# A graph network, linear attention and expert layer on one core: a rebuilt opening, token-major denominators, rotating sum banks

## The reference

```
xn = layernorm(x)
x  = x + gnn(xn) + mix(xn)
x  = x + ffn(layernorm(x))

gnn: xg = layernorm(xn) * norm_g + norm_b
     out1 = gat(xg, W1, 4 heads x 192);  out2 = gat(out1, W2, 2 heads x 96)
     return concat(xn, out2) @ Wu + bu
gat: h = x @ W;  e = leaky_relu(h.a_src[src] + h.a_dst[dst]);  softmax over the edges of each dst
     out[dst] = sum(alpha * h[src]) + bias
mix: q, k = elu(xn @ Wq + bq) + 1, elu(xn @ Wk + bk) + 1;  v = xn @ Wv + bv   (12 heads of 64)
     kv = sum_n k v;  z = 1 / (q . sum_n k);  return (q kv z) @ Wo + bo
ffn: top 2 of 8 experts, each 768 -> 384 -> 768 with gelu, weighted by the gate scores
```

## Time and profile before

| | us |
|---|---|
| three runs | 1069.29, 1074.53, 1076.05 |
| median of the runs | 1074.53 |
| profiled execution, its own time | 1070.59 |
| its span in the profile | 1068.8 |
| mean granted PE clock | 0.948 of 2.4 GHz |
| PE busy | 933.8 (87%) |
| DVE busy | 774.0 (72%) |
| ACT busy | 344.1 (32%) |

### The profile page before, as it was taken

The page is one execution under the profiler, slowest core; times in us unless marked ns, Lnnn a source line. Parts: engine busy times, 40 slices in busy tenths (PEclk is TensorE's granted clock), DMA queues, the critical chain, the costliest instruction groups (busy, mean ns, idle before and its releaser), DMA issues.

```text
span 1068.8 us, 16945 instructions
## 1 busy us (share of the span) xinstructions
PE 933.8 (87%) x6241; PEld 675.4 (63%) x6241; DVE 774.0 (72%) x1740; ACT 344.1 (32%) x424; POOL 134.6 (13%) x139
## 2 busy tenths in 40 slices
PE   3699999999889899979978988967888569999994
PEld 2666666666454455546668988947775446666662
DVE  6568789897765786986587987689989944444442
ACT  3561122122225232432332433314435532222220
POOL 3010000000001000000000000000601035555541
PEclk9889999999999999999989999988899779999997
DMA  8340222135352745627787100006026757778761
GB/s 236 121 163 11 80 66 77 66 121 222 134 193 84 247 163 185 210 84 240 237 330 317 50 1 1 1 1 264 3 92 256 271 179 176 189 186 192 188 165 18
DMA packets 61451, 155.44 MB, mean 145 GB/s; under 512 B 11940, under 2 KB 31270, under 8 KB 58426
## 3 DMA queue, kind: packets, MB, share of 16 engines
q1 hardware_dynamic: 48586, 112.33, 30.1%
q0 software_dynamic: 9936, 34.23, 13.0%
q10 hardware_dynamic: 2848, 7.77, 1.9%
HBM read 108.34 MB, written 48.94 MB: 147 GB/s over the span
## 4 chain that ended last, share of the span: by engine, by line
PE 65%; DVE 22%; DMA 4%; issue 4%; ACT 2%; DVEq 1%; SPq 1%; POOLq 0%
PE PS L1774 40%; PE PS L2017 13%; DVE arena L1517 3%; DVE arena L1473 3%; PE PS L1850 3%; DVE arena L1479 2%; PE PS L2168 2%; PE PS L1830 1%; DVE arena L1489 1%; DVE arena L1379 1%; DMA arena<-in_L_gnn_W_dram 1%; DMA arena<-as_d 1%; PE PS L1861 1%; DVE arena L1275 1%; DVE arena L1223 1%
## 5 line engine op out<-in xcount | busy, mean ns | idle before, releaser
L1774 PE MATMUL PS<-arena 128*128 128x384 f16 (+7 forms) x3396 | 564.6, 322 | 4.8 <-DVE arena L1764 3.0
L1774 PEld LDWEIGHTS PS<-arena 128*128 128x128 f16 (+2 forms) x3396 | 320.7, 99 | 214.3 <-issue 13.5
L2017 PE MATMUL PS<-arena 128*128 128x193 f32 (+1 forms) x1200 | 191.4, 323 | 21.9 <-DVE arena L1479 16.5
L2017 PEld LDWEIGHTS PS<-arena 128*128 128x128 f32 x1200 | 186.9, 200 | 26.4 <-DVE arena L1479 16.0
L1033 ACT ACTIVATE arena<-arena,AS 128x1280 f32<-128x1280 f32 x60 | 81.8, 1363 | 134.9 <-DVE arena L1473 134.7
L1473 DVE SCALAR_TENSOR_TENSOR arena<-arena,AS 128x1280 f32<-128x1280 f32 x60 | 94.2, 1573 | 0.0
L1479 DVE SCALAR_TENSOR_TENSOR arena<-arena 128x1280 f32<-128x1280 f32 x60 | 90.6, 1510 | 3.4 <-PE PS L2017 3.3
L1275 DVE TENSOR_SCALAR arena<-arena 128x240 f16<-128x240 f16 x324 | 89.2, 275 | 0.0
L1274 DVE TENSOR_SCALAR arena<-arena 128x128 f16<-128x128 f16 x324 | 80.2, 248 | 0.1
L1763 DVE SCALAR_TENSOR_TENSOR arena<-PS,arena 128x768 f32<-128x768 f32 x27 | 25.8, 957 | 62.1 <-PE PS L1774 62.1
L1110 ACT ACTIVATE arena<-PS 128x1536 f16<-128x1536 f16 x27 | 39.1, 1449 | 75.7 <-PE PS L2168 75.7
(11 more groups left out here) (268 smaller groups left out, 915.2 us busy)
## 6 DMA issues: line engine op xcount, KB each, us to landing
arena<-in_L_ffn_W_dram SPq DMA_DIRECT2D x48, 384.0 KB, 3.8
fr_d<-arena SPq DMA_DIRECT2D x48, 384.0 KB, 3.5
arena<-fr_d SPq DMA_DIRECT2D x16, 1152.0 KB, 14.5
arena<-in_x_dram SPq DMA_DIRECT2D x18, 384.0 KB, 5.4
arena<-rr_d SPq DMA_DIRECT2D x4, 1280.0 KB, 8.0
g_d<-arena SPq DMA_DIRECT2D x10, 388.0 KB, 2.5
acc_d<-arena SPq DMA_DIRECT2D x10, 384.0 KB, 2.6
xf_d<-arena ACTq DMA_DIRECT2D x10, 384.0 KB, 3.2
```

The costliest lines, as they stand in the source:

```text
L1774: m = T.matmul(out, left[i][x], right[i][y], start=first and i + r == 0, stop=last and 3 * i + r == n - 1)
L2017: m = T.matmul(ps[b][:, r * (C + 1):(r + 1) * (C + 1)], PT[i % deep][:, d * P:(d + 1) * P], feats, start=t == 0 and r == 0, stop=t == NT - ...
```

## The change

In words:

- SP issues W1's first half before it waits for anything, then the edges, x tile 0, W1's second half, x tile 1, W2 with the logit vectors, x tiles 2 and 3, the small columns, Wk, and tiles 4 to 9.
- POOL makes the constants first, then blanks `CT`, then writes the identity on its diagonal (DVE did that at line 1181).
- PE turns W1 in eight groups, four per half, ahead of the window keys, and makes first products 0 to 3 around the keys and the others four ahead of the turned tiles. The bias products are spread: two after every second tile, the last two inside K's first tile. They use banks 6 and 7, the first products banks 4 and 5.
- ACT loads its table for the square root at the start; DVE takes statistics of two tiles ahead of the keys, not four.
- Every split of Wk, Wv, Wq and Wu is made in CUTS = 3 pieces.
- Denominators token-major: the six steps multiply a 128x128 block of Q (left operand) with two columns (`kcol`), so a chunk's result is [128 tokens x (tiles x 12)]; DVE takes the reciprocal of that, splits it in three bf16 parts, PE turns them (`den_turned`) and DVE copies them to `rparts`. The maxima of a chunk's last step move behind it.
- The sums of layer 1 use banks (5 h + b) mod 8 for head h, and `head_result` comes one unit later.

The core of the diff:

```
@@ sync
+            w1_half(0, s_w1_in)
             sp.wait_ge(s_edges_blank, 1)
...
-            for t in range(4):
-                x_tile(t)
-            sp.dma_start(W1S, W1.rearrange("(k p) n -> p k n", p=P)).then_inc(s_w1_in, 16)
-            for t in range(4, XS):
-                x_tile(t)
+            x_tile(0)
+            w1_half(1, s_w1b_in)
+            x_tile(1)
             sp.dma_start(W2A[:, :, 0:CW], W2.rearrange("(k p) n -> p k n", p=KS)).then_inc(s_w2_in, 16)
...
+            for t in range(2, 4):
+                x_tile(t)
...
             weight(0, Wk)
-            for t in range(XS, NT):
+            for t in range(4, NT):
                 x_tile(t)
-            sp.wait_ge(s_stage_low, 1)
+            sp.wait_ge(s_stage_low, CUTS)
             weight(1, Wv)
@@ gpsimd
-            g.memset(reg(O_X, NT * DCOL // 2), 0.0).then_inc(s_ct_blank, 1)
             const(g.memset(ident[:, :], 0.0))
...
             const(g.memset(zrow, 0.0))
+            g.memset(reg(O_X, NT * DCOL // 2), 0.0).then_inc(s_ct_blank, 1)
+            pool.wait_ge(s_ct_blank, 1)
+            for t in range(NT):
+                i = g.tensor_copy(CT[:, t, t * P:(t + 1) * P], ident[:, :])
+            i.then_inc(s_ct_blank, 1)
@@ scalar
+            for t in range(NT):
+                if t + 2 < NT:
+                    std(t + 2)
+                xn_high(t)
+                if t + 2 < NT:
+                    normed(t + 2)
+                if t + AHEAD < 2 * KC:
+                    m_out(t + AHEAD)
+                if 4 <= t < 4 + CUTS:
+                    high(0, t - 4)
@@ vector
+            for t in range(NT):
+                if t + 3 < NT:
+                    row_stats(t + 3)
+                if t + 2 < NT:
+                    inverse(t + 2)
+                if t + 3 < NT:
+                    variance(t + 3)
+                if t + 2 < NT:
+                    shift(t + 2)
+                if t == 0:
+                    dve.wait_ge(s_window_psum, 2)
+                    V.tensor_copy(kc[:, 0, :, :], ps[6][:, 0:EJ * NU]...).then_inc(s_keys_ready, 1)
+                if 5 <= t < 5 + CUTS:
+                    stage_low(0, t - 5)
...
                 if t == 0:
-                    stage_low(1)
+                    for q in range(CUTS):
+                        stage_low(1, q)
...
-            for j in range(KC):
-                V.tensor_scalar(kones[:, j, :], kones[:, j, :], ksum[:, j:j + 1], None, ALU.mult)
+            for half in range(2):
+                s = slice(64 * half, 64 * half + 64)
+                V.tensor_copy(kcol[s, :, half], ksum[s, :])
...
-                for c in conv_of_t[t0]:
-                    conv_low(c)
-                dve.wait_ge(s_den_psum, n + 1)
-                link(V.reciprocal(recip[:, 0:w], ps[2][:, 0:w]))
-                link(V.tensor_copy(rparts[:, 0:w], recip[:, 0:w]))
...
+                dve.wait_ge(s_den_psum, 2 * n + 1)
+                heads = recip[:, 0:nt, :]
+                link(V.reciprocal(heads, ps[2][:, 0:nt * 2 * KC]...))
+                for r in range(3):
+                    part = rcols[:, 0:nt, 2 * KC * r:2 * KC * (r + 1)]
+                    k = V.tensor_copy(part, heads)
+                    if r < 2:
+                        link(k)
+                        link(V.tensor_tensor(heads, heads, part, ALU.subtract))
+                k.then_inc(s_den_ready, 1)
+                for c in conv_of_t[t0]:
+                    conv_low(c)
+                maxima1(late_maxima[0:1])
+                dve.wait_ge(s_den_psum, 2 * n + 2)
+                V.tensor_copy(rparts[:, 0:w], ps[2].bitcast(BF16)[:, 2 * P:2 * P + w]).then_inc(s_den_ready, 1)
+                maxima1(late_maxima[1:])
...
-                    if t == 1 and h:
+                    if t == 2 and h:
                         head_result(h - 1, CW, 0)
@@ tensor
+            for t in range(NT):
+                turned(t)
+                if t + AHEAD < 2 * KC:
+                    first_product(t + AHEAD)
+                if t == 0:
+                    pe.wait_ge(s_keys_ready, 2)
+                    pe.wait_ge(s_small_in, 80)
+                if t % 2:
+                    norm_bias(t // 2)
...
-                m = T.matmul(ps[2][:, 0:w], kones[:, j, :], QT[:, j, 0:w], start=j == 0, stop=j == KC - 1)
+                for t in range(w // P):
+                    at_t = 2 * KC * t + 2 * j
+                    m = T.matmul(ps[2][:, at_t:at_t + 2], QT[:, j, t * P:(t + 1) * P], kcol[:, j, :], start=True, stop=True, ...)
...
+            def den_turned(n):
+                pe.wait_ge(s_den_ready, 2 * n + 1)
+                for t in range(CH[n][1] // P):
+                    m = T.transpose(ps[2].bitcast(BF16)[:, (2 + t) * P:(3 + t) * P], rcols[:, t, :], identb[:, :])
+                m.then_inc(s_den_psum, 1)
...
                     if t == 0 and r == 0 and h:
-                        pe.wait_ge(s_head_out, 5 * (results + h - 1) + b + 1)
-                    m = T.matmul(ps[b][:, r * (C + 1):(r + 1) * (C + 1)], PT[i % deep][:, d * P:(d + 1) * P], feats,
+                        if C != CW:
+                            pe.wait_ge(s_head_out, 5 * (H1 + h - 1) + b + 1)
+                        elif b >= 3:
+                            pe.wait_ge(s_head_out, 5 * (h - 1) + b - 2)
+                        elif h >= 2:
+                            pe.wait_ge(s_head_out, 5 * (h - 2) + b + 3)
+                    m = T.matmul(ps[sum_bank(h, b) if C == CW else b][:, r * (C + 1):(r + 1) * (C + 1)], PT[i % deep][:, d * P:(d + 1) * P], feats,
```

More of the change, by code:

```diff
@@ L529, in group_of, with sum_bank @@
             return [t < b for _, b in GROUPS].index(True)
-        def copies_of(s):
-            return range(s - 4, s - 3) if s < NT + 2 else range(2 * s - NT - 6, 2 * s - NT - 4)
         def rows_bank(i):
             return 5 if i == 1 else 0
+        def sum_bank(h, b):
+            return (5 * h + b) % 8
         def turn_bank(t):
@@ L771, in _ @@
             select(g.memset(bd, 0.0))
-            select(g.memset(kones, 0.0))
-            heads = kones.rearrange("p j (g m) -> p j g m", g=4)
-            for j in range(KC):
-                for half in range(2):
-                    i = g.memset(heads[64 * half:64 * half + 64, j, :, 2 * j + half:32:12], 1.0)
-            select(i)
+            select(g.memset(kcol, 0.0))
+            select(g.memset(rcols, 0.0))
             pool.wait_ge(s_small_in, 96)
@@ L929, in _ @@
             act.wait_ge(s_keys_ready, 2)
-            high(1)
+            for q in range(CUTS):
+                high(1, q)
             for t in range(NT):
@@ L973, in _ @@
                 if t == 3:
-                    high(2)
+                    for q in range(CUTS):
+                        high(2, q)
                 for c in conv_of_g[t]:
@@ L1003, in mask_half @@
                              ACT.Relu, bias=bigc[:, :], scale=-BIG).then_inc(s_mask_ready, 1)
-            high(3)
+            for q in range(CUTS):
+                high(3, q)
             for n, (c0, w) in enumerate(CH):
@@ L1164, in _ @@
             row_stats(0)
-            for s in range(1, 4):
-                row_stats(s)
-                variance(s - 1)
-            inverse(0)
-            variance(3)
-            shift(0)
-            inverse(1)
-            shift(1)
+            row_stats(1)
+            variance(0)
+            variance(1)
             dve.wait_ge(s_const_ready, CONST)
             dve.wait_ge(s_window_psum, 1)
-            V.tensor_copy(kc[:, 1, :, :], ps[5][:, 0:EJ * NU].rearrange("p (j u) -> p j u", j=EJ))
+            V.tensor_copy(kc[:, 1, :, :], ps[7][:, 0:EJ * NU].rearrange("p (j u) -> p j u", j=EJ))
             link(V.tensor_copy(ebase[0:1, :], ps[6][0:1, 0:NU]))
@@ L1178, in _ @@
             V.tensor_copy(lefti[0:1, 0:1], left[0:1, 0:1]).then_inc(s_left_ready, 1)
-            dve.wait_ge(s_ct_blank, 1)
-            for t in range(NT):
-                i = V.tensor_copy(CT[:, t, t * P:(t + 1) * P], ident[:, :])
-            link(i)
+            inverse(0)
+            inverse(1)
+            shift(0)
+            shift(1)
+            row_stats(2)
+            variance(2)
+            dve.wait_ge(s_ct_blank, 2)
             dve.wait_ge(s_left_ready, 1)
@@ L1339, in _ @@
                 if t in (5, 6, 7):
[L1340 to L1345 removed]
+                    stage_low(2, t - 5)
                 for c in conv_of_g[t]:
@@ L1400, in _ @@
                     if i == 0:
-                        stage_low(3)
+                        for q in range(CUTS):
+                            stage_low(3, q)
                     for c in conv_of_j[i]:
@@ L1482, in head_result @@
                 dve.wait_ge(s_agg, unit0 + (h + 1) * NT)
-                acc = PS[:, 0:5 * 512].rearrange("p (a b) -> p a b", a=5)
-                link(V.reciprocal(rden[:, :, :], acc[:, :, C:2 * C + 2:C + 1]))
+                acc = PS.rearrange("p (a b) -> p a b", a=8)
+                first = sum_bank(h, 0) if C == CW else 0
```

(13 more changed lines are left out.)

184 lines of the change are left out of this document (83 added, 101 removed).

## The result

| | before | after |
|---|---|---|
| four runs, median (us) | 1072.69 | 1042.78 |
| lowest and highest | 1069.29, 1076.05 | 1040.11, 1044.75 |
| profiled execution, its span | 1070.59, 1068.8 | 1042.59, 1040.8 |
| mean granted clock | 0.948 | 0.943 |

The ratio is 0.9715, with a 95% interval of 0.9691 to 0.9738: 29.9 us less by the medians, 28.0 less between the two profiled executions. The forecast was 1045.5.

What follows compares the result with a forecast made beforehand. PE was taken to bound the kernel (65% of the span, DVE 22%), leaving its idle and low-clock time to win. 6.0 + 1.0 + 5.9 + 2.1 - 0.1 + 9.8 + 2.4 = 27.1 us, from 1072.6 to 1045.5 us; range 1037 to 1057.

Steps and rivals of the forecast that it cites:

- Opening, 6.0: Opening up to the K bias: it begins at 73.8 instead of 80.64, 6.8 us less 0.8, so 6.0 us won.
- so I add 0.8: Opening, ahead of the turned tiles: 0.8 us added for a low clock after PE's idle 4 to 5 us.
- 11.8 us after Wv's issue: Opening, behind Wv: bias rows and columns are in 11.8 us after Wv's issue, 65.8 for an issue at 54.
- the same sum gave 75.9: Opening, K bias: the same sum for the kernel before gave 75.9, with the bias waited on for PE until 80.64.
- Head selectors, 1.0: Head selectors on DVE: six operations of 1.26 us become two small copies, 1.0 us won (0 to 1.2).
- Denominators, 5.9 + 2.1 - 0.1: Denominators: PE's waits ahead of the shared products go, winning 5.9 us in chunk 0, 2.1 in chunk 1, -0.1 in chunk 2.
- rival (d): Denominators: each small product waits for the one ahead, eating 28 us; 1073.5 and above, chance 0.02.
- Rotating banks, 9.8 + 2.4: Layer 1's changes of head: three pauses of 3.25 us go, 9.8 us, plus 2.4 us counted for low clock.
- rival (b): Head change: DVE misses its 0.2 us reserve for unit 2; heads give 6, not 12.2: 1051.7, chance 0.08.
- (a): Opening gives nothing: Wv's issue comes at 60 and the K bias again at 80; 1051.5, chance 0.14.
- (c): Opening, x tiles: the clock stays at its lower level, 20 us on top; 1066, chance 0.04.
- The exclusive lock: Opening, edge work: POOL's blanking blocks DVE's first edge operation until 10.6; with ports only shared, 2 us earlier.

Runs made afterwards that it cites:

- e10: Changed kernel with 12 and 30 unused identity transposes filling PE's two pauses ahead of the keys; 1040.12 us.
- e4: Changed kernel with the two bias rows and two bias columns issued ahead of Wv instead of behind it; 1039.94 us.
- e1: Changed kernel with the whole denominator change undone (feature-major, long reciprocal, maxima of the last step ahead), selectors undone too; 1055.46 us.
- e8: Changed kernel with its small denominators, but maxima of a chunk's last step and the conversions ahead of the reciprocal again; 1048.91 us.
- e9: Changed kernel with the old feature-major denominators and long reciprocal, but conversions and maxima kept behind the reciprocal; 1051.09 us.
- e3: Changed kernel with rotating banks kept, but the head result after the second unit as before, not the third; 1058.59 us.
- e5: Changed kernel with POOL's blanking of the histogram ahead of the constants again, as in the kernel before; 1044.59 us.
- e6: Changed kernel with POOL's blanking of the histogram cut into ten pieces; 1044.69 us.
- e11: Changed kernel with bias rows and columns issued early, Wv loaded in thirds, and POOL's blanking ahead of the constants; 1035.65 us.
- e12: Changed kernel with bias rows and columns early, Wv in thirds, unused filler transposes on PE, and Wk's splits spread out; 1032.69 us.

## Why the prediction was right, step by step

The sum said 27.1; the two profiled executions differ by 28.0 and the medians by 29.9.

- **Opening, 6.0: too much, it was 4.1.** Right were W1's transposes (begun at 6.47), the hold by POOL (until 10.0, forecast 10.6), tiles at 5.26 us a pair and ACT's 3.6 us in tiles 4 to 6. The edge work ended at 16.5 and the keys came at 24.4, earlier than the forecast 18.0 and 26.4. The low clock, for which "so I add 0.8" stands, cost more: it was at 0.50 to 0.53 from 18 to 32 us, and products 2 and 3 took 5.3 us instead of 2.7; e10 shows its price. The two errors cancel, and the turned tiles began at 30.3, as the sum had it (29.6 and 0.8). What was too small lies behind: from there to Wv's issue it took 25.2 us and not 23.6 (24.4 in e10), and "11.8 us after Wv's issue" was 13.0, since the column b2 was issued 2.5 us behind Wv and landed at 68.6. So the K bias stood at 76.55 and not 73.8. Of these 2.8 us 0.8 came back: the V product for which it had been taken off took 3.08 us, the length at the full clock. That this landing was what DVE waited for, as the prediction put it, e4 shows.
- **The opening's check and its spread.** The check by the kernel before, "the same sum gave 75.9", was none: 52.64 and 19.8 make 72.4, and there DVE's one-hots waited for the last x tiles (until 67.5 us), not for the landing. By the five other traces of this opening the gain is 3.7 to 5.6 us, so up to 1.5 of the missing 1.9 may be chance.
- **Head selectors, 1.0:** 0.8; the two copies are one row of 0.34 us.
- **Splits elsewhere, 0:** nothing separates them in the trace. Not tried alone.
- **Denominators, 5.9 + 2.1 - 0.1:** 6.0 and 2.4 in the trace; 5.3 and 2.6 when undone in e1. The eight records of four small products take 0.95 us (row 347.00) for the 0.92 that line 2048 gave, so rival (d) is out. What the prediction had not seen: the reserve is 1.9 us (copy done at 355.94, used at 357.83), and in chunk 0 the order of the maxima is worth as much as the small reciprocal (e8, e9).
- **Rotating banks, 9.8 + 2.4:** the pauses as said, 3.3 us each in e3. Layer 1 is 14.2 us shorter, so the clock gave 4.4, and 2.4 were counted. 1.3 of the 4.4 come from a place that was left out, a low stretch at the start of layer 1, which cost 2.6 us before (544 to 552) and 1.3 after (530 to 534); the other 3.1 lie within the bound of 3.4. The reserve of 0.2 us for unit 2 was real (0.04 at 604.72), and rival (b) came close.
- **Not in the sum:** two stretches of low clock, 1.7 us each, at 292 and 326. They went though PE's work and waits in those places are the same. Every one of the twelve other variants has at least one of the two, and e1, e5, e6 and e10 have both. One at 466 is new and took 1.7. So 1.7 us net and the 2.0 more in layer 1 stood in for the 1.9 missing in the opening and for what was lost behind layer 1 (1.4): the mechanisms came as told, and that the total fits to 1 us is luck in part.
- **Rivals:** (a) did not come, though 2 us of it did. (c) did not: the clock was at 1.00 from 32 to 56 us, over nine of the ten tiles. It fell again for the last tile, the last bias products and the first K product (0.50 over 56 to 62), which cost nothing, since DVE waited for the column until 68.6. The rule behind (c), that transposes do not count as PE-busy in the same way (the Trainium skill, "TensorE: Matmul & The Clock Gate", the part on PE-mode transpose), is not borne out by e10: transposes alone, f32 ones against the identity, filled PE from 21 to 24.5 us, and the clock stayed at 1.00. It is not refuted either, since in e5 the clock stayed at 1.00 over an empty pause.
- **The exclusive lock** (the Trainium skill, "SBUF — State Buffer", the section on the shared port pair): the trace agrees. The operation took 2.61 us under one long blanking, 0.42 without it, and 0.8 to 0.95 against pieces, with POOL longer by 1.2 us in turn.

## What to carry to other kernels

Free banks won nothing until the work queued on DVE ahead of PE's next need was moved too (e3), and of the denominators' 7.9 us the order alone won 2.8 for no new layout (e9); look at the order first. Issue small late loads ahead of a large one that has to wait, and load a large one in the parts in which its place comes free. A total moves by 1.7 us with each stretch of low clock, so read a gain of a few us from the offset of one instruction between two traces, not from the end.

## What was not expected of the hardware

- Behind the edge work with PE half idle (14 to 17 us) the granted clock fell at 18 and stayed low until 32 us although PE was busy again from 25 on. In the eight other variants that keep the constants first and leave the pauses empty it also fell, but at 17 to 24 us and for 7 to 14 us in all, with nearly the same work; in the two with filled pauses (e10, e12) it stayed at 1.00.
- A pause of 2.63 us let it fall in e11 and not in e5, after the same products (e11's transposes had two pauses of 0.2 us more). What decides it stays open.
- Cutting a POOL blanking in ten does not free DVE: both engines slow down while they overlap, DVE by some 0.45 us an operation, and DVE's chain ends at the same time as with one hold.
- 60 small f32 products of two columns (120 records) cost PE no more than the 18 wide ones (36 records) that they replace: 4.97 us from one step of a chunk to the next against 5.02.
